# Groups of 124 nodes in place of 126 in the first edge stage of a two-layer graph network

## The reference

```python
q, k, v = x_norm @ Wq.T + bq, x_norm @ Wk.T + bk, x_norm @ Wv.T + bv
dk, dv  = silu(edge_attr @ Wdk.T + bdk), silu(edge_attr @ Wdv.T + bdv)
attn = silu(sum(q[dst] * k[src] * dk, axis=1)) * cosine_cutoff(edge_weight)
msg  = v[src] * dv * attn[:, None]
agg  = segment_sum(msg, dst, num_segments=N)
out  = x + agg @ Wo.T + bo
```

## Time and profile before

| | |
|---|---|
| median of 3 runs | 3775.6 us (3765.82 to 3777.75) |
| the profiled execution | 3789.33 us |
| its span, first to last instruction | 3787.5 us, 113,336 instructions |
| mean granted TensorE clock | 0.959 of full speed |
| busy share of the span | PE 91%, DVE 87%, ACT 74%, PEld 73%, POOL 65% |
| DMA queues, share of 16 engines | 47.9% indirect (POOL's queue), 31.9% plain (SP's queue) |
| bytes moved | 915.39 MB, mean 242 GB/s |
| `prepare` | to about 62 us |
| `nodes_0` | about 62 to 240 us |
| `edges_0` | about 240 to 1440 us, 216 chunks |
| second layer | from there to the end |

### The profile page before, as it was taken

One profiled execution on the slowest core, in us unless ns is written; L12 is line 12 of the kernel. 1 busy time (PEld: TensorE's weight loads), 2 busy tenths in 40 slices (PEclk: granted clock), 3 DMA queues, 4 the chain that ended last, 5 costly groups with the idle time before them and its releaser, 6 DMA issues. The chain is left out here.

```text
span 3787.5 us, 113336 instructions
## 1 busy us (share of the span) xinstructions
PE 3442.8 (91%) x25474; PEld 2765.5 (73%) x25475; DVE 3283.3 (87%) x10411; ACT 2816.1 (74%) x8685; POOL 2448.1 (65%) x2605
## 2 busy tenths in 40 slices
PE   3978999999999997996999999999999999997997
PEld 2547777777777775774777777777777777776986
DVE  6768999999999995664899998999999999996775
ACT  2856777777777774553889888889889998885553
POOL 2656777777777773554566666666666666663776
PEclk8989999999999998998899999999999999998998
DMA  3879999999999994776888887888888888875664
GB/s 107 255 225 303 296 298 299 298 299 299 294 299 298 295 263 158 262 261 220 234 234 236 236 227 218 231 230 235 230 226 237 236 236 233 231 228 149 214 204 134
DMA packets 613511, 915.39 MB, mean 242 GB/s; under 512 B 210712, under 2 KB 422794, under 8 KB 612916
## 3 DMA queue, kind: packets, MB, share of 16 engines
q0 software_dynamic: 168160, 579.41, 47.9%
q1 hardware_dynamic: 445268, 335.07, 31.9%
HBM read 739.98 MB, written 177.47 MB: 242 GB/s over the span
## 5 line engine op out<-in xcount | busy, mean ns | idle before, releaser
L905 POOL DMA_INDIRECT kv<-kv_table,rec x864 | 887.5, 1027 | 293.6 <-issue 269.9
L1572 POOL DMA_INDIRECT kv1c<-kv_table,rec x912 | 877.4, 962 | 285.4 <-issue 262.4
L1617 ACT ACTIVATE wv<-kv1c,wv 128x64 f32<-128x64 f32 x3648 | 904.0, 334 | 16.0
L1680 DVE CUSTOM_DVE_ANT_0 masked_scores<-score_p,far 126x384 f32<-126x384 f32 x1216 | 604.6, 553 | 62.7 <-issue 28.5
L943 ACT ACTIVATE gates<-gates_p 128x512 f32<-128x512 f32 x864 | 465.5, 591 | 78.9 <-PE gates_p L1074 76.6
L1772 PE MATMUL sum_p<-wv,hot 128*126 128x260 f32 x1824 | 519.7, 424 | 2.3 <-ACT wv L1617 2.3
L1737 PE MATMUL qe_p<-qrel,hotT 126*128 126x256 f32 x1824 | 464.9, 392 | 26.1 <-ACT hotT L1602 18.0
L1094 PE MATMUL sum_p<-msg,hot_weighted 128*126 128x256 f32 x1728 | 432.2, 393 | 5.3 <-ACT hot_weighted L951 5.3
L1737 PEld LDWEIGHTS qe_p<-qrel,hotT 126*128 126x128 f32 x1824 | 363.8, 200 | 88.2 <-ACT hotT L1602 19.3
L1772 PEld LDWEIGHTS sum_p<-wv,hot 128*126 128x126 f32 x1824 | 339.8, 200 | 86.6 <-issue 3.8
L1582 POOL TENSOR_TENSOR faded<-acc,fade 126x260 f32<-126x260 f32 x304 | 189.2, 622 | 329.6 <-ACT fade L1625 324.1
(11 more groups left out here) (285 smaller groups left out, 7230.6 us busy)
## 6 DMA issues: line engine op xcount, KB each, us to landing
key<-segment_keys SPq DMA_DIRECT2D x304, 189.0 KB
q_blk<-q_table SPq DMA_DIRECT2D x216, 256.5 KB
acc_table<-acc SPq DMA_DIRECT2D x304, 128.0 KB
qrel<-q_by_relation SPq DMA_DIRECT2D x304, 126.0 KB
feat<-in_edge_feat_t SPq DMA_DIRECT2D x216, 128.0 KB
agg_and_x_plus_h<-total SPq DMA_DIRECT2D x216, 126.0 KB
kv1c<-kv_table,rec POOLq DMA_INDIRECT x912
kv<-kv_table,rec POOLq DMA_INDIRECT x864
```

The lines of the kernel that those rows point to most:

```text
L905: pool.indirect_dma_start(kv[it.slot(AHEAD)][:, t, :], None, c["kv0_d"], bass.IndirectOffsetOnAxis(ap=rec[k][:, t, 0:1].bitcast(I32), axis ...
L1572: pool.indirect_dma_start(kv[k][:, t, :], None, c["kv1_d"], bass.IndirectOffsetOnAxis(ap=rec[k][:, t, 0:1].bitcast(I32), axis=0)).then_inc ...
L1617: ins = act.activation(wv[k][:, t, h, 0:DK], kv[s][:, t, D + h * DK:D + (h + 1) * DK], ACT.Copy, scale=wv[k][:, t, h, DK:DK + 1])
L1680: dve.tensor_tensor_reduce(junk[k][:, h], score_p[:, :, h, :], far[it.slot(4)][:], 1.0, -BIG, ALU.subtract, ALU.max, top[s][:, h:h + 1]).t ...
```

## The change

`GROUP` becomes 124, and there are 51 groups; `SUBS` stays at 300 sub-ranges of 21 for the second layer. As 124 is not a multiple of 21, the ranges of the groups are no longer made from those of the sub-ranges: they get a fourth column of their own in the tables of `prepare`, so there are eight indirect gathers on POOL in place of six, and four columns in place of three in each comparison. The six small operations on DVE that made group ranges from sub-ranges go. The one-hot matrices for the sort come 17 at a time in place of 10 (`LANE_STEP`). Padding lanes of the sort read node N - 1, and the table of sums is read up to N rows, not NP.

```diff
 SUB = 21
 SEG = SUB * RELS
-PER_GROUP = 6
-GROUP = SUB * PER_GROUP
+GROUP = 124
 GROUPS = -(-N // GROUP)
-SUBS = GROUPS * PER_GROUP
+SUBS = 300
...
-SUB_ROWS, SUB_COLS = 100, 3
+RANGE_ROWS, SUB_COLS, RANGE_COLS = 100, 3, 4
+RANGES = RANGE_ROWS * RANGE_COLS
...
-        LANE_STEP = 10
+        LANE_STEP = 17
...
-                    for col in range(SUB_COLS):
+                    for col in range(RANGE_COLS):
                         pool.indirect_dma_start(
...
-                dve.tensor_scalar(who[:, :, 0], who_p[:], float(NOBODY), float(NP - 1), ALU.add,
+                dve.tensor_scalar(who[:, :, 0], who_p[:], float(NOBODY), float(N - 1), ALU.add,
                                   ALU.min).then_inc(who_ready, 1)
...
-                dve.tensor_copy(c["lo1"][:, 0:SUBS], lo_f)
-                dve.tensor_reduce(lo0_f[:], lo_f.rearrange("o (g j) -> o g j", j=PER_GROUP), AX, ALU.min)
-                link(dve.tensor_reduce(hi0_f[:], hi_f[:].rearrange("o (g j) -> o g j", j=PER_GROUP), AX, ALU.max))
-                dve.tensor_copy(c["lo0"][:, 0:GROUPS], lo0_f[:])
-                link(dve.tensor_tensor(hi0_f[:], hi0_f[:], lo0_f[:], ALU.subtract))
+                dve.tensor_copy(c["lo1"][:, 0:SUBS], lo_f[:, of_subs])
+                dve.tensor_copy(c["lo0"][:, 0:GROUPS], lo_f[:, of_groups])
...
-        acc_rows = c["acc_d"].rearrange("(n r) f -> n (r f)", r=RELS)[0:NP, :]
+        acc_rows = c["acc_d"].rearrange("(n r) f -> n (r f)", r=RELS)[0:N, :]
```

More of the change, by code:

```diff
@@ L55 @@
 Q_ROW = 2 * D + 1
-SUB_ROWS, SUB_COLS = 100, 3
+RANGE_ROWS, SUB_COLS, RANGE_COLS = 100, 3, 4
+RANGES = RANGE_ROWS * RANGE_COLS
 BATCHES = NP // P + TYPES
 NOBODY = 1 << 13
-assert SUB_ROWS * SUB_COLS == SUBS and REAL_PARTS * PER_PART == E
+assert RANGE_ROWS * SUB_COLS == SUBS and SUBS * SUB >= N and REAL_PARTS * PER_PART == E
+assert GROUPS <= RANGE_ROWS and SUBS * SUB <= NP
 class Item:
@@ L187, in build @@
         ident = keep("ident", [P, P])
-        iota = keep("iota", [P, GROUP])
+        iota = keep("iota", [P, SEG])
         eps, one, minus_big = keep("eps", [P, 1]), keep("one", [P, 1]), keep("minus_big", [P, 1])
@@ L241, in prepare @@
         outer = sb("outer", [P, 2, REAL_PARTS])
[L242 to L251, removed]
+        bounds = sb("bounds", [RANGE_ROWS, 2, RANGE_COLS])
+        full = sb("full", [RANGE_ROWS, 2, RANGE_COLS])
+        row_of = sb("row_of", [RANGE_ROWS, 2, RANGE_COLS], I32)
+        fine = sb("fine", [RANGE_ROWS, 2, RANGE_COLS, ROW])
+        partial = sb("partial", [RANGE_ROWS, 2, RANGE_COLS])
+        edge_range = sb("edge_range", [RANGE_ROWS, 2, RANGE_COLS])
+        row = sb("row", [1, 2, RANGES])
+        lo_f, hi_f, len_f = row[:, 0, :], sb("hi_f", [1, RANGES]), sb("len_f", [1, RANGES])
+        of_subs, of_groups = slice(0, SUBS), slice(SUBS, SUBS + GROUPS)
         total = sb("total", [1, 2])
@@ L274, in prepare @@
         ends_p = ctx.enter_context(nc.psum_tensor("ends_p", [P, 2, REAL_PARTS], F32))
-        row_p = [ctx.enter_context(nc.psum_tensor(f"row_p{a}", [1, SUBS], F32)) for a in range(2)]
+        row_p = [ctx.enter_context(nc.psum_tensor(f"row_p{a}", [1, RANGES], F32)) for a in range(2)]
         loaded, consts_loaded = sem("prep_loaded"), sem("prep_consts")
@@ L301, in _ @@
                 sp.dma_start(order[:], w0["order"]).then_inc(consts_loaded, 16)
-                sp.dma_start(begin[:], w0["begin"]).then_inc(consts_loaded, 16)
-                sp.dma_start(c["iota"][:], w0["iota"].to_broadcast([P, GROUP])).then_inc(consts_loaded, 16)
+                sp.dma_start(bounds[:].rearrange("p a c -> p (a c)"), w0["bounds"]).then_inc(consts_loaded, 16)
+                sp.dma_start(c["iota"][:], w0["iota"].to_broadcast([P, SEG])).then_inc(consts_loaded, 16)
                 sp.wait_ge(reach_ready, 2)
@@ L353, in _ @@
                 for a in range(2):
-                    for col in range(SUB_COLS):
-                        ins = pe.matmul(row_p[a][:, col * SUB_ROWS:(col + 1) * SUB_ROWS],
-                                        edge_range[:, a, col:col + 1], c["ident"][0:SUB_ROWS, 0:SUB_ROWS],
+                    for col in range(RANGE_COLS):
+                        ins = pe.matmul(row_p[a][:, col * RANGE_ROWS:(col + 1) * RANGE_ROWS],
+                                        edge_range[:, a, col:col + 1], c["ident"][0:RANGE_ROWS, 0:RANGE_ROWS],
                                         start=True, stop=True)
@@ L431, in _ @@
                 dve.tensor_scalar(reach[:, 1, :], inner[:, 1, :], carry[:, 1:2], None, ALU.min).then_inc(reach_ready, 1)
-                link(dve.tensor_scalar(end[:], begin[:], float(SUB), None, ALU.add))
                 dve.tensor_tensor_scan(outer[:, 0, :], ends[:, 0, :], ends[:, 0, :], -1.0, ALU.max, ALU.max)
@@ L435, in _ @@
                 link(dve.tensor_tensor_scan(outer[:, 1, :], back, back, 1e9, ALU.min, ALU.min))
-                for a, bound, op in ((0, begin, ALU.is_lt), (1, end, ALU.is_ge)):
-                    for col in range(SUB_COLS):
-                        link(dve.tensor_scalar(junk[0:SUB_ROWS, 0, 0:REAL_PARTS], outer[0:SUB_ROWS, a, :], bound[:, col:col + 1], 0.0,
+                for a, op in ((0, ALU.is_lt), (1, ALU.is_ge)):
+                    for col in range(RANGE_COLS):
+                        link(dve.tensor_scalar(junk[0:RANGE_ROWS, 0, 0:REAL_PARTS], outer[0:RANGE_ROWS, a, :],
+                                               bounds[:, a, col:col + 1], 0.0,
                                                op, ALU.add, accum_out=full[:, a, col:col + 1]))
@@ L469, in _ @@
                                       ALU.is_equal).then_inc(in_lane_ready, 1)
[L471 to L474, removed]
+                dve.wait_ge(fine_got, 16 * 2 * RANGE_COLS)
+                for a, op in ((0, ALU.is_lt), (1, ALU.is_ge)):
+                    for col in range(RANGE_COLS):
+                        link(dve.tensor_scalar(junk[0:RANGE_ROWS, 0, 0:ROW], fine[:, a, col, :], bounds[:, a, col:col + 1], 0.0,
                                                op, ALU.add, accum_out=partial[:, a, col:col + 1]))
@@ L488, in _ @@
                 link(dve.tensor_tensor(len_f[:], hi_f[:], lo_f, ALU.subtract))
-                dve.tensor_copy(c["lo1"][:, 0:SUBS], lo_f)
-                dve.tensor_reduce(lo0_f[:], lo_f.rearrange("o (g j) -> o g j", j=PER_GROUP), AX, ALU.min)
-                link(dve.tensor_reduce(hi0_f[:], hi_f[:].rearrange("o (g j) -> o g j", j=PER_GROUP), AX, ALU.max))
-                dve.tensor_copy(c["lo0"][:, 0:GROUPS], lo0_f[:])
-                link(dve.tensor_tensor(hi0_f[:], hi0_f[:], lo0_f[:], ALU.subtract))
+                dve.tensor_copy(c["lo1"][:, 0:SUBS], lo_f[:, of_subs])
+                dve.tensor_copy(c["lo0"][:, 0:GROUPS], lo_f[:, of_groups])
                 m0, m1 = CH0 // MINI, CH1 // MINI
                 a0, a1 = c["n0"][:, 0:GROUPS], c["n1"][:, 0:SUBS]
-                link(dve.tensor_scalar(a0, hi0_f[:], float(m0 - 1), None, ALU.add))
+                link(dve.tensor_scalar(a0, len_f[:, of_groups], float(m0 - 1), None, ALU.add))
                 link(dve.tensor_scalar(a0, a0, m0.bit_length() - 1, None, ALU.arith_shift_right))
                 link(dve.tensor_scalar(a0, a0, 1.0, None, ALU.max))
-                link(dve.tensor_scalar(a1, len_f[:], float(m1 - 1), None, ALU.add))
+                link(dve.tensor_scalar(a1, len_f[:, of_subs], float(m1 - 1), None, ALU.add))
                 link(dve.tensor_scalar(a1, a1, 5, None, ALU.arith_shift_right))
@@ L982, in one_hot @@
                     dve.scalar_tensor_tensor(hot[it.slot(4)][:],
-                                             c["iota"][:].rearrange("p (o n) -> p o n", o=1).to_broadcast([P, T0, GROUP]),
+                                             c["iota"][:, 0:GROUP].rearrange("p (o n) -> p o n", o=1).to_broadcast([P, T0, GROUP]),
                                              first_of(s), rec[s][:, :, 1:2].to_broadcast([P, T0, GROUP]),
@@ L2193, in device_arrays @@
     par1[0, :, :, 2] = -BIG
+    bounds = np.empty((RANGE_ROWS, 2, RANGE_COLS), np.float32)
+    for end in range(2):
+        bounds[:, end, 0:SUB_COLS] = SUB * (np.arange(SUBS).reshape(SUB_COLS, RANGE_ROWS).T + end)
+        bounds[:, end, SUB_COLS] = GROUP * (np.arange(RANGE_ROWS) + end)
     spread_head = np.zeros((P // 4, HEADS, SEG), np.float32)
@@ L2212, in device_arrays @@
         "ident": np.eye(P, dtype=np.float32),
-        "iota": np.arange(GROUP, dtype=np.float32)[None, :],
+        "iota": np.arange(SEG, dtype=np.float32)[None, :],
         "lane": np.arange(P, dtype=np.float32)[None, :],
@@ L2219, in device_arrays @@
                                                1).astype(np.float32)),
-        "begin": np.ascontiguousarray((SUB * np.arange(SUBS, dtype=np.float32)).reshape(SUB_COLS, SUB_ROWS).T),
+        "bounds": bounds.reshape(RANGE_ROWS, 2 * RANGE_COLS),
         "w_o": f("L0_gnn_Wo").T,
```

## The result

The changed kernel takes 4262.94 us (median of 5 runs, 4255.35 to 4284.13), against 3777.75 us of the kernel before, measured alongside: the ratio is 1.1288, with a 95% interval of 1.1257 to 1.1318. It is slower by 13%. The forecast was 4105 us, within 3860 to 4320. The time lies in the range, but more than half of what was lost lies in a stage that the forecast had left at nothing.

A forecast was written before the change was run, and what follows sets the result against it. Compute was taken to pace `nodes_0` and `edges_0`, with DMA close behind. Fewer chunks -42.5, `prepare` +4, `nodes_0` +193 and `edges_0` +178 made +332 us on the median 3775.6: about 4105 us, range 3860 to 4320.

The forecast's parts named there:

- Four engines: Transfers of a group's 124 rows would run on 4 DMA engines, 31 rows each, in place of 14 with 9 each.
- rotating: Rival: the four engines change from one transfer to the next; `nodes_0` stays paced by PE; 3838 us, chance 0.08.
- no concentration: Rival: transfers of 124 rows run on 13 to 16 engines, only the fewer chunks count; 3740 us, chance 0.07.
- `nodes_0`: Stage paced by four full engines, 7.0 us an item against 3.02: +193 us, from +91 to +265.
- `edges_0`: Stage slowed by its store on four engines, 6.2 us a chunk against 5.31: +178 us, 0 to +398, besides fewer chunks.
- The fewer chunks: In `edges_0`, 208 chunks in place of 216, eight less at 5.31 us: -42.5 us.
- two bounds: In `edges_0`, the four engines' time and the chain of stores; from both, 6.2 us a chunk, between 5.31 and 7.3.
- The bound from the engines' time: In `edges_0`, the store's added time on four engines gives 5.80 to 6.24 us a chunk, or 5.31 if waiting gives way.
- The chain of stores: In `edges_0`, each store of `total` waits for the landing of the one before, which will take 3.1 to 8.0 us.
- hidden in `edges_0`: Rival: the four engines fill their gaps, the landing stays under 5.3 us, DVE keeps the pace; 3930 us, chance 0.15.
- `edges_1` keeps its 126 rows and 304 chunks: The second layer's edge stage has unchanged shapes and was forecast to differ by 0 us.
- `prepare`: Early loads on four engines, more comparisons on DVE and a later `who_p`: +4 us, 2 to 8.

The follow-up runs named there:

- the four executions above: Profiled executions of the changed kernel and of three runs that leave `nodes_0` as it is: 339, 330, 328 and 327 us in that stage.

## Why the prediction was right, and where it was not

**Four engines: right.** Every count of completions says so, and the packets in flight in `nodes_0` and the spread of its transfers show that they are the same four. The rivals "rotating" and "no concentration" fall.

**`nodes_0`: right mechanism, term over-sized.** +160 us in place of +193 (+148 to +160 by the four executions above). The item was priced at 7.0 us with 20.4 GB/s an engine; it took 6.2, which is 143.4 KB at 23 GB/s. The rate was read from stretches in which all 16 engines were busy, or from five engines with rows of 800 bytes; four engines with rows of 1 and 2 KB and little beside them ran faster.

**`edges_0`: the gain right, the loss over-sized.** The fewer chunks were to give -42.5 us; `edges_0` with the full pace gives -53: the last eight intervals between stores, those with empty chunks, also shrank from 48 to 40 us, which fits two such chunks in place of four. The pace was put at 6.2 us a chunk from two bounds, and took 5.6. The operations with 124 columns or rows took a few ns less, as was said: 388 ns in place of 390 for `hot_weighted`, 734 in place of 739 for `hot`. The bound from the engines' time failed: with the 93.7% busy counted as work it gave 5.80 to 6.24 us. Its own reserve, that part of the busy time is waiting that gives way, fits the 5.6, but no run shows it by itself. The chain of stores was the right place: SP waits for the landing in 76 of 107 chunks, and the landing lies in the range that was given for it (3.1 to 8.0 us), but at 5.3 us in the mean it is only as long as a chunk, so most of it stays hidden. DVE and PE idle by a twentieth there, not by the tenth that was named as a sign. The rival "hidden in `edges_0`", at 3930 us, was closer: the changed kernel with DVE's loop moved takes 3945.85.

**`edges_1`: wrong.** "`edges_1` keeps its 126 rows and 304 chunks" was true and was taken for "keeps its time". The step that failed is the one that never stood there: the stage was put at nothing, without a look at what the change does to the place of later code in each engine's program. DVE's list was looked at for its shapes and not for its length. DVE's loop stands 20 instructions later, and some 8 us a turn in 36 turns are the 296 us. That the time still fell into the range is chance: of the 332 us forecast 165 came, in the stages named, and 296 came in one that was not.

**`prepare`:** +2 us in place of +4. (The sum on the median is 4107.6 us; "about 4105" is a rounding of it.)

## What to carry to other kernels

Before a row count is changed, work out how many engines each transfer will use, from its completion packets in the trace and from its divisors: here 128, 126, 125, 124, 112, 100 and 12 rows ended with 16, 14, 5, 4, 16, 10 and 12 small packets, and a transfer of 128 rows, with four that nobody reads (x) or that a later store overwrites (`total`), was better than one of 124: `edges_0` took 1140 us against 1197, and `nodes_0`, with its other stores split, 204 against 339. When a stage slows that the change doesn't touch, look at the instruction queue first (230 packets against 55 here), and at an engine that idles right behind a loop's branch (DVE, 5.10 and 2.64 us); then shift the loop by some dead instructions, which tells code from data in one run. An edit ahead of a long loop, in the same engine's program, moved it in either direction here: 20 instructions on DVE made the stage 16% longer (1955 us against 1680), and 40 took the loss away in the changed kernel (1667 against 1975).

## What the runs showed of the hardware that was not expected

- A loop of 274 DVE instructions costs 8 us more a turn, or nothing, by where it begins: 1661 to 1680 us or 1955 to 1983 us for the stage over all runs, with 55 to 57 or 230 to 231 packets of code. The one slow place that was tried again 128 instructions further on was slow there too.
- A store that goes to four full engines holds up SP in its issue: 1.6 to 3.3 us, mostly about 2.0, in place of 0.32.
- Each of four full engines, with the other twelve nearly idle, moved 23 GB/s in rows of 1 and 2 KB, against 17.6 to 20.4 where all 16 were busy.
